# A fourth even unit moved by DMA, loads paced one behind each move, and the sum first in each turn of VectorE

## The chip, the core and the metric

The kernel runs on one core of one Trainium2 chip. A core has TensorE (PE, matrix products, with its weight loads shown as PEld), VectorE (DVE), ScalarE (ACT), GpSimd (POOL) and SyncE (SP), whose queue issues nearly all DMAs here. The metric is the device time of one execution in microseconds; the median of several executions is compared.

## The reference, cut to what matters

`x` is 2048 x 512, `adj` is 2048 x 2048, both float32.

```python
h = relu(layernorm(x))                        # layer 0
weight_q = quantised(normalised(weight))      # integers, -7 to 7
support = relu(quantised(h) @ weight_q)       # quantised again to integers, 0 to 15
x = x + c_out * (adj @ support_q)
h = relu(layernorm(x))                        # layer 1
S = (adj + adj.T) * 0.5 + eye
d = where(S.sum(axis=1) > 0, S.sum(axis=1) ** -0.5, 0)
x = x + (adj @ (d[:, None] * S * d[None, :])) @ h
```

The kernel computes the last line as `adj @ (d * (S @ (d * h)))`. The sums of S over its rows need both the row sums and the column sums of `adj`.

## The kernel before, in words

`adj` is read in 32 units of 128 rows x 1024 columns, 512 KB each. Unit u is half u % 2 of row block u // 2. TensorE needs the transposed matrix in SBUF (`at`), in float16 as a high and a low half: high = float16(256 a), low = float16(256 a - high). A unit gets there in one of two ways.

A *turned* unit goes over TensorE: `turn(u)` (L1029) makes eight transposes into a PSUM bank pair (`ps_a` and `ps_b` in alternation), ScalarE writes the high half from PSUM (`hi_turned`, L479), and VectorE takes a column sum from PSUM and writes the low half (`turned_out`, L845, with L702 and L715). ScalarE also takes the row sum in a pass of its own (`row_sum`, L462).

A *moved* unit is split before it is transposed: ScalarE writes the high half into a stage and takes the row sum on the way (`hi_rows`, L469, L476), VectorE writes the low half into the stage (`lo_rows`, L718, L720), and SP issues a DMA transpose of each from the stage to `at` (`move`, L315, L323). There are two pairs of stages, and `hi_rows` of one moved unit waits until the unit two before it has landed. All odd units from 3 to 29 and the even ones in `EVEN` (14, 18, 22) are moved. The column sums of odd units are made from a sum that GpSimd adds up in `acc` (L435 to L444), each add behind the product of some row block; those of moved even units are late column sums (L708), a VectorE pass over 2048 columns of `at`.

The first product (L1045, `layer0`) makes 16 row blocks of `adj @ support_q`; a block r is 16 column blocks with two matmuls each, and needs units 2r and, from column block 8 on, 2r + 1. It goes into one of two banks, `ps_p[r % 2]`, so block r waits until VectorE has emptied the bank of block r - 2: `x1_tile(r - 2)` (L834, L840), which adds the product to x and takes the statistics (L842, L843) for the second layer norm.

The order of the work is written out by hand. Each engine runs a loop over turns r = 1 to 13 (PE L1097, ACT L586, DVE L903, SP L355). `TURNS[r]` lists the units that TensorE turns ahead of or within block r, `MOVES[r]` those that are moved in it. In turn r VectorE does `turned_out` of the first turned unit, then `x1_tile(r - 1)`, then `lo_rows` of the first moved unit, then the rest. SP's queue is in order: it waits for the halves of a unit, issues the two transposes, and loads come between. Units 14 to 19 are loaded in one go (L353), units 20 to 23 behind the move of unit 7 (L361); from turn 8 on a load comes ahead of a move and one behind it. After the first product TensorE runs the second product (two sweeps, L1140) and the third (L1153).

Of the kernel before, what the change touches and what calls it, by code (L numbers as in the profile page):

```python
# [11 lines left out]
W = N // 2  # L12
# [11 lines left out]
GROUPS = (0, 2, 4, 8, 12, T)  # L24
LATE_GROUPS = (0, 13, T)
LATE_SUMS = (0, 2)
EVEN = (14, 18, 22)
MOVED = tuple(sorted(tuple(range(3, 30, 2)) + EVEN))
ADDED = tuple(range(1, 30, 2))
TURNED = tuple(u for u in range(UNITS) if u not in MOVED)  # L30
# [3 lines left out]
def gnn_kernel(nc, x, adj, adj_scale, weight, wgt_alpha, act_alpha, act_alpha2, out):  # L34
# [5 lines left out]
    with ctx:  # L40
# [6 lines left out]
        def sem(name):  # L47
            return ctx.enter_context(nc.semaphore(name))
# [41 lines left out]
        def late(tile, off, cols, dt):  # L90
            v = at[:, tile * PAIR + off:tile * PAIR + off + cols * (2 if dt == f32 else 1)]
            return v.bitcast(f32) if dt == f32 else v
# [2 lines left out]
        w_int = late(13, 2048, KD * D, f16)  # L95
        acc = late(15, 0, W, f32)

        def stage(u, lo):

            if u == 29:  # L100
                return late(15, 2048 + lo * W, W, f16)
            return late(14, 2048 * (MOVED.index(u) % 2) + lo * W, W, f16)
        xq = [late(12, 1024 * k, 2 * D, f16) for k in range(2)]
        sq = [late(11, 1024 * k, 2 * D, f16) for k in range(2)]
        hT = [late(10, 1024 * k, 2 * D, f16) for k in range(2)]
# [73 lines left out]
        acc_done = sem("acc_done")  # L179
        hi_ready = sem("hi_ready")  # L180
        lo_ready = sem("lo_ready")
        at_moved = [[sem(f"at_moved{k}{lo}") for lo in range(2)] for k in range(2)]
        atlo = sem("atlo")
        prod_done = sem("prod_done")
        x1_ready = sem("x1_ready")
# [84 lines left out]
        TURNS = {r: [2 * r + 4] for r in range(2, 12)}  # L270
        TURNS.update({1: [4, 6], 12: [28, "acc"], 13: [30, 31]})


        ROW_SUMS = {2: [0, 1], 4: [2, 4], "acc": []}


        MOVES = {r: [2 * r + 7] for r in range(2, 12)}
        MOVES[1] = [7, 9]
        for u in EVEN:
            MOVES[u // 2 - 4].append(u)  # L280
            TURNS[u // 2 - 2] = []

        def wait_moved(engine, u):
            k = MOVED.index(u)
            for lo in range(2):
                engine.wait_ge(at_moved[k % 2][lo], 16 * (k // 2 + 1))


        def arrivals(u):
# [2 lines left out]
        @block.sync  # L292
        def _(sp):
            def load_x(n):
                sp.dma_start(feat3[:, 2 * n:2 * n + 2, :], x_tiles[:, 2 * n:2 * n + 2, :]).then_inc(x_in[n], 16)

            def rows(u):
                sp.dma_start(unit_in(u), adj[(u // 2) * P:(u // 2 + 1) * P, (u % 2) * W:(u % 2 + 1) * W])\
                  .then_inc(arr_sem(u), 16)

            def rows_again(u):
                free_slot(before(u))
                rows(u)

            def free_slot(u):

                if u in ADDED:
                    sp.wait_ge(acc_done, ADDED.index(u) + 1)
                if u in MOVED:
                    sp.wait_ge(lo_ready, MOVED.index(u) + 1)  # L310
                else:
                    sp.wait_ge(turned, turn_no(u) + 1)
                    sp.wait_ge(rs_done, TURNED.index(u) + 1)

            def move(u):  # L315
                for lo, ready in ((0, hi_ready), (1, lo_ready)):
                    sp.wait_ge(ready, MOVED.index(u) + 1)
                    if u == 29:
                        wait_moved(sp, 25)
                        wait_moved(sp, 27)  # L320
                    elif u >= 12:
                        free_slot(waited_in(u)[lo])
                    sp.dma_start_transpose(at_half(u // 2, lo, u % 2).rearrange("p (b i) -> p b i", i=P), stage(u, lo))\  # L323
                      .then_inc(at_moved[MOVED.index(u) % 2][lo], 16)

            def store_x1(t):
                sp.wait_ge(x1_ready, t + 1)
                sp.dma_start(out_tiles[:, t:t + 1, :], feat3[:, t:t + 1, :]).then_inc(x1_stored[t], 16)

            def sums(v):  # L330
                h, j = v // T, v % T
                sp.dma_start(sum_in(v), adj[j * P:(j + 1) * P, h * W:(h + 1) * W]).then_inc(sum_arrival(v), 16)

            for h in range(2):
                sp.dma_start(w_raw[:, 2 * h * D:2 * (h + 1) * D].rearrange("p (k d) -> p k d", d=D),
                             weight.rearrange("(k p) d -> p k d", p=P)[:, 2 * h:2 * h + 2, :]).then_inc(w_in[h], 16)
            for n in range(2):
                load_x(n)
            rows(0)
            rows(1)  # L340
            for n in range(2, T // 2):
                load_x(n)
            for u in range(2, 12):
                rows(u)
            sums(0)
            sums(1)
            sp.wait_ge(hT_ps, T // 2)
            rows(12)
            rows(13)
            move(3)  # L350
            move(5)
            sp.wait_ge(sq_ready, T // 2)
            for u in range(14, 20):  # L353
                rows(u)
            for r in range(1, 12):  # L355
                if r >= 8:
                    rows_again(2 * r + 9)
                for u in MOVES[r]:
                    move(u)
                    if u == 7:  # L360
                        for w in range(AHEAD, AHEAD + 4):  # L361
                            rows_again(w)
                if r >= 8:
                    rows_again(2 * r + 8)
            for v in range(2, 6):
                free_slot(UNITS - 6 + v)
                sums(v)
            for t in range(13):
                store_x1(t)
            for v in range(6, UNITS):  # L370
                if v in (6, 7, 8):
                    store_x1(v + 7)
                sp.wait_ge(slo, v - 3)
                sums(v)

            sp.wait_ge(z_ps, 2 * B)
            for k in range(4):
                for t in range(4 * k, 4 * k + 4):
                    sp.wait_ge(x1_stored[t], 16)
                sp.dma_start(feat3[:, 4 * k:4 * k + 4, :], out_tiles[:, 4 * k:4 * k + 4, :]).then_inc(x1_back[k], 16)  # L380
            for t in range(T - 1):
                sp.wait_ge(y_out, t + 1)
                sp.dma_start(out_tiles[:, t:t + 1, :], feat3[:, t:t + 1, :]).then_inc(out_stored, 16)
            for h in range(2):
                sp.wait_ge(y_out, T + h)
                sp.dma_start(out_tiles[:, T - 1:T, h * DH:(h + 1) * DH], feat3[:, T - 1:T, h * DH:(h + 1) * DH])\
                  .then_inc(out_stored, 16)
            sp.wait_ge(out_stored, 16 * (T + 1))

        @block.gpsimd  # L390
        def _(pool):
# [42 lines left out]

            for k, u in enumerate(ADDED):  # L435
                pool.wait_ge(arr_sem(u), arrivals(u))
                if u > 5:
                    pool.wait_ge(prod_done, next(r for r in MOVES if u in MOVES[r]))
                if k == 0:
                    pool.wait_ge(lo_ready, 2)  # L440
                    nc.gpsimd.tensor_scalar(acc, unit_in(u), 0.0, 1.0, ALU.add, ALU.mult).then_inc(acc_done, 1)
                else:
                    pool.wait_ge(acc_done, k)
                    nc.gpsimd.tensor_tensor(acc, acc, unit_in(u), ALU.add).then_inc(acc_done, 1)  # L444

        @block.scalar
        def _(act):
# [21 lines left out]
            def hi_rows(u):  # L469
                k = MOVED.index(u)  # L470
                act.wait_ge(arr_sem(u), arrivals(u))
                if k < 2:
                    act.wait_ge(w_ready, 2)
                else:
                    wait_moved(act, MOVED[k - 2])
                nc.scalar.activation(stage(u, 0), unit_in(u), ACT.Copy, scale=SA, accum_out=rowsum[:, u:u + 1])\  # L476
                  .then_inc(hi_ready, 1)

# [10 lines left out]

            def turn_hi(u):  # L490
                if u == 28:
                    wait_moved(act, 25)
                    wait_moved(act, 27)
                elif u == 30:
                    wait_moved(act, 29)
                if u != "acc":
                    hi_turned(u)
# [83 lines left out]
            scale_support(7)  # L581
            hi_turned(2)
            hi_rows(5)
            for w in ROW_SUMS[2]:
                row_sum(w)
            for r in range(1, 14):  # L586
# [38 lines left out]
        def _(dve):  # L625
# [204 lines left out]
            clamp_support(7)  # L830
            lo_turned(2)
            lo_rows(5)

            def x1_tile(r):  # L834

# [66 lines left out]

            for r in range(1, 14):  # L903
                now = TURNS[r]
                for u in now[:1]:
                    turned_out(u)
                x1_tile(r - 1)
                moves = MOVES.get(r, [])
                for u in moves[:1]:
                    lo_rows(u)  # L910
# [1 line left out]
                    turned_out(u)  # L912
                for u in moves[1:]:
                    lo_rows(u)
                if r - 4 in LATE_SUMS:
                    column_sum_late(r - 4)
                for k, u in enumerate(EVEN):
                    if r == (7, 9, 12)[k]:
                        wait_moved(dve, u)
                        column_sum_late(u)  # L920
                if r == 8:
# [286 lines left out]
```

## Time and profile before

| | us |
|---|---|
| median of 3 runs | 499.73 (499.46 to 500.01) |
| the profiled execution | 499.41 |
| its span | 497.5 |
| TensorE busy | 482.9 |
| VectorE busy | 275.2 |
| ScalarE busy | 136.0 |
| GpSimd busy | 46.5 |

The span is the time from the first to the last instruction of the program that the profile shows; the profiled execution's own time lies 1.9 us above it. Times of rows count from the span's start. The granted TensorE clock is full in every slice. The first product, with the preparation of the matrix, ends at about 162 us; the second runs to about 328, the third to the end.

### The profile page before, as it was taken

The numbers are of one execution on the slowest core, as the hardware profiler recorded it, in microseconds if no ns is written. First come the engines' busy times: TensorE is split into PE (matmuls) and PEld (weight loads), VectorE is DVE, ScalarE is ACT, GpSimd is POOL, SyncE is SP. The second block draws the span as 40 slices with busy tenths as digits, with TensorE's granted clock in tenths as the row PEclk, the third lists the DMA queues.
The fourth block names the chain that finished last, engine by engine and source line by source line (L and its number), as shares of the span: only waits on it lengthen the run. The fifth ranks groups of instructions, "written<-read, shape, count | busy, mean of one in ns | idle before, by whom it ended". The sixth has DMA issues, their size and how long they took to land.

```text
span 497.5 us, 6362 instructions
## 1 busy us (share of the span) xinstructions
PE 482.9 (97%) x2390; PEld 236.6 (48%) x2390; DVE 275.2 (55%) x367; ACT 136.0 (27%) x192; POOL 46.5 (9%) x54
## 2 busy tenths in 40 slices
PE   3999998999999999999999999999999999999997
PEld 2755554445554444444444444444444444444446
DVE  6964969989999688785996777340000000000000
ACT  1796634433432343534512122140000000000000
POOL 2322932332200000000000000000000000000000
PEclk9999999999999999999999999999999999999999
DMA  8978996779677233233223231045010000100001
GB/s 296 402 315 191 303 243 130 130 172 208 152 216 288 65 106 124 87 107 104 86 89 122 88 123 42 1 134 224 22 42 21 21 21 21 42 21 21 22 21 43
DMA packets 54731, 60.56 MB, mean 122 GB/s; under 512 B 37688, under 2 KB 37944, under 8 KB 54712
## 3 DMA queue, kind: packets, MB, share of 16 engines
q1 hardware_dynamic: 54704, 60.30, 40.5%
q8 instruction: 12, 0.20, 0.2%
q14 instruction: 7, 0.06, 0.0%
q10 hardware_dynamic: 8, 0.00, 0.0%
HBM read 42.99 MB, written 8.39 MB: 103 GB/s over the span
## 4 chain that ended last, share of the span: by engine, by line
PE 84%; DVE 7%; DMA 3%; SPq 2%; ACT 1%; issue 1%; POOL 0%; ACTq 0%; DVEq 0%; POOLq 0%
PE ps_a L1163 31%; PE ps_p L1062 13%; PE ps_p L1126 7%; PE ps_a L1126 7%; PE ps_b L1126 7%; PE ps_m L1126 4%; PE ps_h L1126 4%; DMA feat<-in_x 2%; DVE at L720 2%; PE ps_b L1013 1%; PE ps_m L1062 1%; PE ps_h L1062 1%; DVE at L715 1%; DVE small L900 1%; PE ps_b L1179 1%
## 5 line engine op out<-in xcount | busy, mean ns | idle before, releaser
L1062 PE MATMUL ps_p<-small,at 128*128 128x512 f16 x448 | 100.0, 379 | 2.0 <-DVE feat L840 2.0
L982 DVE SCALAR_TENSOR_TENSOR feat<-ps_a,feat 128x512 f32<-128x512 f32 (+1 forms) x16 | 10.8, 676 | 148.7 <-PE ps_a L1163 144.2
L1163 PE MATMUL ps_a<-small,at 128*128 128x512 f16 x360 | 80.2, 379 | 0.0
L1163 PE MATMUL ps_a<-a_in,at 128*128 128x512 f16 x360 | 80.2, 379 | 0.0
L1062 PEld LDWEIGHTS ps_p<-small,at 128*128 128x128 f16 x448 | 43.6, 98 | 51.5 <-DVE feat L840 2.5
L551 ACT ACTIVATE split<-a_in 128x1024 f16<-128x1024 f32 x30 | 31.7, 1057 | 101.5 <-PE ps_p L1126 90.0
L1163 PEld LDWEIGHTS ps_a<-a_in,at 128*128 (+1 forms) x360 | 35.2, 98 | 42.5
L1163 PEld LDWEIGHTS ps_a<-small,at 128*128 (+1 forms) x360 | 35.2, 98 | 42.5
L896 DVE TENSOR_TENSOR split<-a_in,split 128x1024 f16<-128x1024 f32 x30 | 36.7, 1224 | 33.7 <-ACT split L551 33.7
L1126 PE MATMUL ps_p<-feat,split 128*128 (+1 forms) x180 | 43.9, 379 | 0.5 <-DVE small L900 0.5
L1126 PE MATMUL ps_a<-feat,split 128*128 (+1 forms) x180 | 43.8, 379 | 0.0
L1126 PE MATMUL ps_b<-feat,split 128*128 (+1 forms) x180 | 43.7, 379 | 0.0
L887 DVE TENSOR_TENSOR a_in<-a_in,at 128x1024 f32<-128x1024 f32 x30 | 36.8, 1226 | 1.0
L886 DVE SCALAR_TENSOR_TENSOR a_in<-a_in,at 128x1024 f32<-128x1024 f32 x30 | 36.5, 1218 | 0.0
L1126 PEld LDWEIGHTS ps_p<-feat,split 128*128 128x128 f16 x180 | 17.5, 98 | 22.0 <-DVE small L900 1.0
L1126 PEld LDWEIGHTS ps_a<-feat,split 128*128 128x128 f16 x180 | 17.6, 98 | 21.4 <-issue 0.5
L1126 PEld LDWEIGHTS ps_b<-feat,split 128*128 128x128 f16 x180 | 17.6, 98 | 21.2
L1126 PE MATMUL ps_m<-feat,split 128*128 (+1 forms) x90 | 24.3, 379 | 0.0
L1126 PE MATMUL ps_h<-feat,split 128*128 (+1 forms) x90 | 24.3, 379 | 0.0
L444 POOL TENSOR_TENSOR at<-at 128x1024 f32<-128x1024 f32 x8 | 21.2, 2648 | 18.4 <-PE ps_p L1062 17.8
L444 POOL TENSOR_TENSOR at<-at,a_in 128x1024 f32<-128x1024 f32 x6 | 15.2, 2537 | 25.4 <-PE ps_p L1062 19.2
L720 DVE SCALAR_TENSOR_TENSOR at<-at 128x1024 f16<-128x1024 f32 x10 | 14.2, 1428 | 4.7 <-ACT at L476 4.7
(179 smaller groups left out, 432.5 us busy)
## 6 DMA issues: line engine op xcount, KB each, us to landing
a_in<-in_adj SPq DMA_DIRECT2D x46, 512.0 KB, 3.9
at<-in_adj SPq DMA_DIRECT2D x16, 512.0 KB, 10.0
out<-feat SPq DMA_DIRECT2D x31, 256.0 KB, 4.2
feat<-in_x SPq DMA_DIRECT2D x8, 512.0 KB, 10.8
feat<-out SPq DMA_DIRECT2D x4, 1024.0 KB, 9.3
at<-in_L_gnn_weight SPq DMA_DIRECT2D x2, 512.0 KB, 3.8
at<-at SPq DMA_TRANSPOSE x34, 3.3
split<-in_adj SPq DMA_DIRECT2D x1, 512.0 KB, 16.2
```

What stands on the lines that cost most here:

```text
L444: nc.gpsimd.tensor_tensor(acc, acc, unit_in(u), ALU.add).then_inc(acc_done, 1)
L551: nc.scalar.activation(part(v % 2, 0), sum_in(v), ACT.Copy).then_inc(shi, 1)
L715: nc.vector.scalar_tensor_tensor(at_half(u // 2, 1, u % 2), turn_bank(u)[:, :], SA, at_half(u // 2, 0, u % 2), ALU.mult, ALU.subtract).the ...
L720: nc.vector.scalar_tensor_tensor(stage(u, 1), unit_in(u), SA, stage(u, 0), ALU.mult, ALU.subtract)\
L886: link(nc.vector.scalar_tensor_tensor(u3, u3, SA, at_across(h, 0, j), ALU.mult, ALU.add))
L887: last = nc.vector.tensor_tensor(u3, u3, at_across(h, 1, j), ALU.add)
L896: nc.vector.tensor_tensor(part(v % 2, 1), sum_in(v), part(v % 2, 0), ALU.subtract).then_inc(slo, 1)
L900: nc.vector.scalar_tensor_tensor(z_part(t, 1), BANK[t % B], cz[:, t:t + 1], z_part(t, 0), ALU.mult, ALU.subtract).then_inc(z_ready, 1)
L982: nc.vector.scalar_tensor_tensor(out, products, 1.0 / (SA * SZ), out, ALU.mult, ALU.add).then_inc(y_out, 1)
L1062: last = nc.tensor.matmul(l0_bank(r), at_block(r, lo, j), small[:, j * D:(j + 1) * D], start=(j == 0 and lo == 0), stop=(j == T - 1 and lo ...
L1126: last = nc.tensor.matmul(BANK[t], part(k, lo)[:, t * P:(t + 1) * P], g_part(j, g_lo), start=(first and lo + g_lo == 0), stop=False)
L1163: last = nc.tensor.matmul(BANK[n], at_block(t, lo, j), z_part(j, z_lo), start=(j == 0 and lo + z_lo == 0), stop=(j == T - 1 and lo == 1))
```

## The change

Unit 10 joins `EVEN`: it is no longer turned (turn 3 has no turned unit) but moved. There are three pairs of stages in place of two, the third in row tile 15 (`stage_no`). Unit 7 is moved ahead of the loop, and the moved units are put anew on the turns: in turns 3 to 7 the even ones come one turn later than before, but for 22. On SP's queue only units 14 and 15 are loaded in one go; each of 16 to 23 is loaded behind one move (`LOADS`). GpSimd's adds keep their turns by a table (`ADD_AT`), the one of unit 7 without a wait for a product; its first waits for the low half of unit 7. ScalarE takes the row sum of unit 1 in turn 1. VectorE does `x1_tile(r - 1)` first in turn r, ahead of `turned_out`, and the late sums of units 0 and 2 come one turn earlier; that of unit 10 is in turn 5.

```diff
-EVEN = (14, 18, 22)
+EVEN = (10, 14, 18, 22)
...
+        def stage_no(u):
+            return (MOVED.index(u) - len(MOVED)) % 3
+
         def stage(u, lo):
-            if u == 29:
-                return late(15, 2048 + lo * W, W, f16)
-            return late(14, 2048 * (MOVED.index(u) % 2) + lo * W, W, f16)
+            k = stage_no(u)
+            return late(14 + k // 2, 2048 * (k % 2 if k < 2 else 1) + lo * W, W, f16)
...
-        ROW_SUMS = {2: [0, 1], 4: [2, 4], "acc": []}
-        MOVES = {r: [2 * r + 7] for r in range(2, 12)}
-        MOVES[1] = [7, 9]
         for u in EVEN:
-            MOVES[u // 2 - 4].append(u)
             TURNS[u // 2 - 2] = []
+        ROW_SUMS = {2: [0], 4: [1, 2, 4], "acc": []}
+        MOVES = {1: [9], 2: [10, 11], 3: [13], 4: [14, 15], 5: [17], 6: [18, 19], 7: [21, 22], 8: [23], 9: [25],
+                 10: [27], 11: [29]}
+        ADD_AT = {u: r for r in MOVES for u in MOVES[r]}
...
             sp.wait_ge(sq_ready, T // 2)
-            for u in range(14, 20):
-                rows(u)
+            rows(14)
+            rows(15)
+            move(7)
+            LOADS = {9: [16], 10: [17], 11: [18], 13: [19], 14: [20], 15: [21], 17: [22], 18: [23]}
             for r in range(1, 12):
                 if r >= 8:
                     rows_again(2 * r + 9)
                 for u in MOVES[r]:
                     move(u)
-                    if u == 7:
-                        for w in range(AHEAD, AHEAD + 4):
+                    for w in LOADS.get(u, []):
+                        if w < AHEAD:
+                            rows(w)
+                        else:
                             rows_again(w)
...
-                if u > 5:
-                    pool.wait_ge(prod_done, next(r for r in MOVES if u in MOVES[r]))
+                if u in ADD_AT:
+                    pool.wait_ge(prod_done, ADD_AT[u])
                 if k == 0:
-                    pool.wait_ge(lo_ready, 2)
+                    pool.wait_ge(lo_ready, 3)
...
-                if k < 2:
+                if k < 3:
                     act.wait_ge(w_ready, 2)
                 else:
-                    wait_moved(act, MOVED[k - 2])
+                    wait_moved(act, MOVED[k - 3])
...
             hi_rows(5)
+            hi_rows(7)
...
             lo_rows(5)
+            lo_rows(7)
...
             for r in range(1, 14):
                 now = TURNS[r]
+                x1_tile(r - 1)
                 for u in now[:1]:
                     turned_out(u)
-                x1_tile(r - 1)
...
-                if r - 4 in LATE_SUMS:
-                    column_sum_late(r - 4)
+                if r - 3 in LATE_SUMS:
+                    column_sum_late(r - 3)
                 for k, u in enumerate(EVEN):
-                    if r == (7, 9, 12)[k]:
+                    if r == (5, 7, 9, 12)[k]:
```

## Rows read from the trace of the kernel before

**Rows 1.** The page: busy time of each engine, and the chain that ended last.

```profile
PE 482.9 (97%) x2390; PEld 236.6 (48%) x2390; DVE 275.2 (55%) x367; ACT 136.0 (27%) x192; POOL 46.5 (9%) x54
...
PE 84%; DVE 7%; DMA 3%; SPq 2%; ACT 1%; issue 1%; POOL 0%; ACTq 0%; DVEq 0%; POOLq 0%
```

**Rows 2.** Waits of TensorE: total us, times, longest.

```profile
PE ps_p L1062 <- DVE feat L840: 2.0, 1, 2.0
...
PE ps_p L1126 <- DVE small L900: 0.5, 1, 0.5
```

**Rows 3.** Timeline of TensorE, 44 to 165: start, us, instruction, idle before.

```profile
61.49 1.04 PE L1041 MATMUL ps_a<-ident,at 128*128 128x128 f32 x8
62.36 7.07 PE L1062 MATMUL ps_p<-small,at 128*128 128x512 f16 x32
...
70.14 7.07 PE L1062 MATMUL ps_p<-small,at 128*128 128x512 f16 x32
79.19 7.08 PE L1062 MATMUL ps_p<-small,at 128*128 128x512 f16 x32 [1.97 <-DVE feat L840]
...
131.93 1.90 PE L1062 MATMUL ps_p<-small,at 128*128 128x512 f16 x8
...
139.72 1.04 PE L1041 MATMUL ps_a<-ident,a_in 128*128 128x128 f32 x8
...
155.28 7.07 PE L1062 MATMUL ps_m<-small,at 128*128 128x512 f16 x32
```

**Rows 4.** Timeline of VectorE, 68 to 80.

```profile
76.12 1.22 DVE L702 TENSOR_REDUCE colp<-ps_b 128x8 f32<-128x1024 f32 x1
...
78.39 0.74 DVE L840 SCALAR_TENSOR_TENSOR feat<-ps_p,cst,feat 128x512 f32<-128x512 f32 x1
```

**Rows 5.** Timeline of ScalarE, 68 to 80.

```profile
71.20 1.06 ACT L476 ACTIVATE at<-at 128x1024 f16<-128x1024 f32 x1 [7.10 <-DMA at<-at]
...
74.86 1.00 ACT L487 ACTIVATE at<-ps_b 128x1024 f16<-128x1024 f32 x1
```

**Rows 6.** SP's queue: timeline, 51 to 64 and 133 to 137; line 323 (ns min/median/max).

```profile
59.02 1.97 SPq L298 DMA_DIRECT2D a_in<-in_adj  x4
61.04 8.07 SPq L323 DMA_TRANSPOSE at<-at  x2
...
135.29 0.52 SPq L298 DMA_DIRECT2D a_in<-in_adj  x1
...
L323 SPq DMA_TRANSPOSE at<-at x34: 1231/1265/6357, 38.0 to 134.0; - x34
...
DMA to landing us min/median/max: 3.0/3.3/9.1
```

**Rows 7.** Lines 708 and 840: ns min/median/max, first and last start.

```profile
L708 DVE TENSOR_REDUCE colp<-at x5: 2277/2279/2280, 81.1 to 140.0; 128x8 f32<-128x2048 f16 x5
...
L840 DVE SCALAR_TENSOR_TENSOR feat<-ps_p,cst,feat x14: 735/742/745, 51.8 to 152.8; 128x512 f32<-128x512 f32 x14
```

**Rows 8.** Stretches: length, then busy us of PE, PEld, DVE, ACT, POOL.

```profile
46.00:102.90 56.90, 54.93 (x279) 27.80 (x278) 46.01 (x48) 27.46 (x46) 28.75 (x12) 1.00 0.89 202
102.90:148.30 45.40, 45.40 (x236) 23.49 (x234) 44.83 (x46) 17.70 (x27) 8.71 (x4) 1.00 0.75 184
```

**Rows 9.** Timeline of VectorE, 44 to 64.

```profile
44.87 1.22 DVE L720 SCALAR_TENSOR_TENSOR at<-at 128x1024 f16<-128x1024 f32 x1
...
53.44 2.49 DVE L720 SCALAR_TENSOR_TENSOR at<-at 128x1024 f16<-128x1024 f32 x1
...
63.12 2.12 DVE L720 SCALAR_TENSOR_TENSOR at<-at 128x1024 f16<-128x1024 f32 x1
```

**Rows 10.** Timeline of GpSimd, 44 to 72.

```profile
52.48 2.37 POOL L444 TENSOR_TENSOR at<-at 128x1024 f32<-128x1024 f32 x1 [0.17 <-POOL at L444]
```

**Rows 11.** Timeline of VectorE, 131 to 149.

```profile
131.13 0.74 DVE L840 SCALAR_TENSOR_TENSOR feat<-ps_p,cst,feat 128x512 f32<-128x512 f32 x1
...
132.73 1.19 DVE L720 SCALAR_TENSOR_TENSOR at<-a_in,at 128x1024 f16<-128x1024 f32 x1
```

**Rows 12.** Waits of ScalarE.

```profile
ACT at L476 <- DMA at<-at: 22.9, 9, 7.1
```

More of the change, by code:

```diff
@@ L181, in gnn_kernel @@
         lo_ready = sem("lo_ready")
-        at_moved = [[sem(f"at_moved{k}{lo}") for lo in range(2)] for k in range(2)]
+        at_moved = [[sem(f"at_moved{k}{lo}") for lo in range(2)] for k in range(3)]
         atlo = sem("atlo")
@@ L271, in gnn_kernel @@
         TURNS.update({1: [4, 6], 12: [28, "acc"], 13: [30, 31]})
-        ROW_SUMS = {2: [0, 1], 4: [2, 4], "acc": []}
-        MOVES = {r: [2 * r + 7] for r in range(2, 12)}
-        MOVES[1] = [7, 9]
         for u in EVEN:
-            MOVES[u // 2 - 4].append(u)
             TURNS[u // 2 - 2] = []
+        ROW_SUMS = {2: [0], 4: [1, 2, 4], "acc": []}
+        MOVES = {1: [9], 2: [10, 11], 3: [13], 4: [14, 15], 5: [17], 6: [18, 19], 7: [21, 22], 8: [23], 9: [25],
+                 10: [27], 11: [29]}
+        ADD_AT = {u: r for r in MOVES for u in MOVES[r]}
         def wait_moved(engine, u):
             k = MOVED.index(u)
+            same = [w for w in MOVED[:k + 1] if stage_no(w) == stage_no(u)]
             for lo in range(2):
-                engine.wait_ge(at_moved[k % 2][lo], 16 * (k // 2 + 1))
+                engine.wait_ge(at_moved[stage_no(u)][lo], 16 * len(same))
         def arrivals(u):
@@ L318, in move @@
                     if u == 29:
-                        wait_moved(sp, 25)
-                        wait_moved(sp, 27)
+                        wait_moved(sp, MOVED[-3])
+                        wait_moved(sp, MOVED[-2])
                     elif u >= 12:
@@ L323, in move @@
                     sp.dma_start_transpose(at_half(u // 2, lo, u % 2).rearrange("p (b i) -> p b i", i=P), stage(u, lo))\
-                      .then_inc(at_moved[MOVED.index(u) % 2][lo], 16)
+                      .then_inc(at_moved[stage_no(u)][lo], 16)
             def store_x1(t):
@@ L491, in turn_hi @@
                 if u == 28:
-                    wait_moved(act, 25)
-                    wait_moved(act, 27)
+                    wait_moved(act, MOVED[-3])
+                    wait_moved(act, MOVED[-2])
                 elif u == 30:
```

## The prediction

> **What bounds the kernel now.** I read the page first. TensorE is busy 482.9 us of a span of 497.5, and the chain that ended last is TensorE for 84% [rows 1]. So time is won only where TensorE has less to do or stops waiting. TensorE's own waits come next: after the first 23 us there are two, 2.0 us in the first product and 0.5 us in the second [rows 2]. The timeline of TensorE puts the 2.0 us wait between the fifth and sixth row blocks of the first product. Block r=4 starts at 70.14. A block is 32 matmuls; from 62.36 to 70.14 lie one block and one turn of 0.87, so it takes 6.91 us (0.216 a matmul). Block 4 therefore ends at 77.05, by the timeline's last end 77.2, and block 5 starts at 79.19 [rows 3].
>
> Why it waits is read backwards from VectorE. Block 5 needs bank r%2, which `x1_tile(3)` frees; that instruction ran at 78.39 [rows 4], although its product was complete at 69.3 (62.36 + 6.91 [rows 3]). In VectorE's program it stood behind the low halves of units 13 and 14 and behind `turned_out(12)`, 76.12 to 78.39 [rows 4]. These waited for ScalarE, where `hi_rows(13)` sat idle for 7.10 us until 71.20 for a stage to come free, with the high half of unit 12 (74.86) behind it [rows 5]. The stage was held by unit 9's transposes: issued from 61.04 on, right behind the four loads of units 20 to 23 issued from 59.02 on, they kept SP's queue for 8.07 us, until 69.1; one transpose is otherwise issued in 1.27 and landed in 3.3 [rows 6]. One long chain, then: four loads ahead of a move, a stage, ScalarE, VectorE, a bank.
>
> **The change part by part.** Each time is the profiled execution's (499.41 us; span 497.5 and 1.9 around it). The median of the runs shown, 499.73, lies 0.32 above it.
>
> *Unit 10 is moved.* TensorE loses the eight transposes of `turn(10)`. From their start to the next matmul is 62.36 - 61.49 = 0.87 us [rows 3] (the 1.04 shown overlaps its neighbour). TensorE is gapless there, so this counts in full: -0.87. ScalarE: `hi_turned` (1.00 for its like) and `row_sum`, a pass of the same width, become one `hi_rows` (1.06) [rows 5]: less. VectorE: `turned_out(10)`, 2.27 from 76.12 to 78.39 for its like [rows 4], becomes `lo_rows` (1.22 [rows 9]) and a late column sum of 2.28 [rows 7]; with the 0.08 by which neighbours overlap, +1.1 us. SP: two more transposes, 1.27 us of issue each [rows 6]; its other issues stay the same in number. Cover: before 102.9, VectorE is idle 56.90 - 46.01 = 10.9 us [rows 8]. If that cover were gone the 1.1 us would land on TensorE.
>
> *The 2.0 us wait.* Two edits act on it, and either seems nearly enough. Loads 16 to 23 now come singly behind moves, so no move lies behind more than two loads; three stage pairs instead of two let ScalarE run one unit further ahead. And `x1_tile(3)` is first in its turn. Working forward from the low half of unit 5 (44.87 to 46.09 [rows 9]), with steps from start to start of 1.1 us for a low half, 1.6 for `x1_tile` with its statistics (131.13 to 132.73 [rows 11]), 2.27 for `turned_out`, 2.2 for a late sum, and with ScalarE's and TensorE's hand-overs where they come later: `lo_rows(7)` ends about 47.2, `x1_tile(0)` 48.8, `turned_out(4)` 51.1; `lo_rows(9)` and `turned_out(6)` end by 56.7, `x1_tile(1)` 58.3, `turned_out(8)` 60.6, the low halves of 10 and 11 by 65.4 (with 2.5 us of waiting for GpSimd in it), `x1_tile(2)` 67.1, low half 13 68.3, late sum 70.5. `x1_tile(3)` frees its bank at 71.3. Block 5 would start at 77.2 - 0.87 = 76.3, so it has 5 us to spare. Gain: -1.97 [rows 3]. From below it could be nothing, if VectorE is late elsewhere (rival 1); more than 1.97 it cannot give, as there is no more idle time there. I take all of it.
>
> *What could be late next.* Unit 10 must be landed at 76.3. Its high half is ready at 57 (ScalarE, behind `hi_turned(8)`), its low at 61.8; two transposes of 3.3 us [rows 6] make 65 (by a worst landing of 9.1, 71). A block reads its odd unit 16 matmuls (3.5 us) after its start. So unit 9: 57.5 against 70.14 - 0.87 + 3.5 = 72.7; before, 71.2 (the end of ScalarE's wait [rows 5]) against 73.6. Unit 11: 68.5 against 79.7. Moves 14 and 18 come one turn later than before, about 80 and 96, for blocks 7 and 9, which start at 91 and 106. Other banks: `x1_tile(2)` at 66.1 for block 4 at 69.3; `x1_tile(5)` at 88.2 for block 7. Their slack is 2.7 us and more even where VectorE runs without a pause. So rows, SP order and the third stage I cost at nothing; each only has to be early. Bounds: -0 to +2.84 together, the latter if one of them gave back everything.
>
> *GpSimd.* `acc` now starts behind the low half of unit 7, about 1.1 us later, and its adds run back to back into the time of the low halves. A row shows what this costs: the low half at 53.44 took 2.49 us against 1.22, while an add of 2.37 us ran from 52.48 to 54.85; one more low half took 2.12, at 63.12 [rows 9, 10]. The Trainium skill, "SBUF — State Buffer", section "SBUF: two separate sides", says that VectorE, in an instruction with two SBUF inputs, and GpSimd take a shared port pair as an exclusive lock, and the loser blocks for the whole of the other's instruction; the row agrees (54.85 plus about 1.1 is 55.93). By that rule up to three more low halves could meet an add before block 7, 3 x 1.3 = 3.9 us of VectorE; by the rows it is two in that stretch. Two (2.5 us) are in the times above, and they leave 5 us free; the sum does not change.
>
> *From 102.9 on.* VectorE is busy 44.83 of 45.40 us [rows 8]: as much a bound as TensorE. `x1_tile(10)` ended at 131.87, and block 12, which needs its bank, began at 131.93 [rows 3, 11]. If TensorE came 2.84 us earlier and VectorE did not, it would wait there. But `x1_tile(10)` now stands ahead of `turned_out(26)` (2.3 us), and VectorE enters this stretch earlier: turn 8 starts with `x1_tile(7)` at 98 to 100 instead of 102.9 with `turned_out(20)`. Carried on without a pause, the pessimistic sum gives `x1_tile(10)` 126.7 against 129.1, and `x1_tile(13)` 150.4 instead of 152.8 [rows 7]; the optimistic one 124 and 148.5. After that block 15 (155.28 + 7.07 = 162.35 before [rows 3]) and `x1_tile(15)` go by TensorE; the second and third products follow it at their old pace.
>
> **Sum.** -0.87 - 1.97 = -2.84. Profiled execution 499.41 - 2.84 = 496.57; from the median 499.73, 496.9.
>
> **Rivals.**
> 1. *VectorE lags, or the bank is still late.* For: its full load after 102.9. Against: 10.9 us of idle before, and `x1_tile` first. Price: 0.5 to 2.3 of the 2.84 comes back, at block 7, 10 or 12: 497.4 to 499.2. "The change doesn't do what it says" is the end of this: only the turn goes, 499.73 - 0.87 = 498.9.
> 2. *The gain is all given back at the turn of unit 30.* The load of unit 30 is issued behind the low move of unit 29, at 135.29 [rows 6], and the turn began at 139.72 [rows 3], some 4.4 us later: it began as its rows came. The low half of unit 29 ends at 133.92 [rows 11]. If it does not end earlier, the turn stays at 139.72 however early TensorE comes: 499.4 to 500.0. Against: VectorE's lead of 2.4 to 4.6 us in the sum above.
> 3. *Slower, by the same place.* If the low half of 29 ends later than 133.92, every microsecond of it is one of the kernel. The added 1.1 us of VectorE work with one or two more collisions of 1.3 us would do it if nothing of the idle time before 102.9 absorbed them: 499.7 + 1.1 = 500.8 to 499.7 + 1.1 + 2.6 = 503.4. For: the late sum and low half of unit 10 go to the busiest engine there; the loads of units 20 to 23, now behind moves 14, 15, 17 and 18, make ScalarE and so VectorE later if one of those moves is. Against: turns 3 to 7 have slack in every step above.
>
> **How the numbers follow.** Forecast: 0.68, with 496.3 to 497.4. Rival 1: 0.15 (faster). Rival 2: 0.09 (same). Rival 3: 0.08 (slower). A change of 0.2%, 1.0 us, is about what a measurement can tell. Faster 0.68 + 0.15 = 0.83. The range runs from 496.2 (the runs differ by 0.3 around the sum) up into rival 1 to 498.8, which leaves out its end and rivals 2 and 3, about 0.2.
>
> **What would show it.** In TensorE's waits the 2.0 us entry on `feat` is gone, and no wait on a DMA or on `feat` above 0.3 us has come. Block 15 ends near 159.5. Transposes number 36, all but the first landing in 3 to 6 us, with no move that keeps SP's queue for 8. ScalarE's wait for moves (22.9 us [rows 12]) falls to a third or less. VectorE shows 6 late column sums (L708's like) where it had 5, and 11 from PSUM where it had 12. Wrong would be: a pause of TensorE before block 7, 10 or 12 (rival 1), or ahead of the turn of unit 30 with VectorE gapless from 100 on (rivals 2 and 3).

## The result, and the profile after

| | median | runs |
|---|---|---|
| before | 499.67 | 498.79 to 502.02 (6) |
| after | 496.88 | 496.19 to 497.05 (6) |

The ratio is 0.9937, interval 0.9919 to 0.9956: 2.8 us faster. The profiled execution took 497.05 with a span of 494.9. Measured a second time, on another chip, it took 496.52 (ratio 0.9952, 0.9938 to 0.9966).

The page, answering to [rows 1]: TensorE has eight transposes less, and the chain is now TensorE for 92% in place of 84%.

```profile
PE 480.7 (97%) x2382; PEld 234.8 (47%) x2382; DVE 275.2 (56%) x367; ACT 134.2 (27%) x191; POOL 45.8 (9%) x54
...
PE 92%; DVE 3%; DMA 2%; ACT 1%; SPq 1%; issue 1%; POOL 0%; ACTq 0%
```

The waits of TensorE, answering to [rows 2]. The 2.0 us on `feat` is gone. The 1.4 us on L695 lies at 20 us, ahead of all that was changed; it was 0.4 in the profile before, and 0.2 to 1.5 in the other profiles below, so it varies from execution to execution.

```profile
PE ps_b L1024 <- DVE at L695: 1.4, 1, 1.4
...
PE ps_p L1137 <- DVE small L911: 0.5, 1, 0.5
```

The timeline of TensorE, 44 to 165, answering to [rows 3]. Blocks 4 and 5 are now one run of 64 matmuls from 69.77, and no line ahead of the second product has an idle time.

```profile
45.56 1.04 PE L1052 MATMUL ps_b<-ident,at 128*128 128x128 f32 x8
...
55.09 13.98 PE L1073 MATMUL ps_p<-small,at 128*128 128x512 f16 x64
68.90 1.04 PE L1052 MATMUL ps_a<-ident,at 128*128 128x128 f32 x8
69.77 13.98 PE L1073 MATMUL ps_p<-small,at 128*128 128x512 f16 x64
...
137.17 1.04 PE L1052 MATMUL ps_b<-ident,a_in 128*128 128x128 f32 x8
...
159.64 1.46 PE L1137 MATMUL ps_a<-feat,split 128*128 128x512 f16 x6
```

I use one measure of this timeline for every kernel below, **the stretch**: from the start of the turn of unit 4 to the first matmul of the second product. It leaves out what single executions do at the start. Before it is 162.19 - 45.06 = 117.13; after, 159.64 - 45.56 = 114.08, and 114.08 again in the second measurement. So 3.05 us went here. (The stretches below are taken from unrounded times, so the last digit can differ by one from the rows.)

VectorE, answering to [rows 4] and [rows 9]: `x1_tile(3)` is at 69.74 instead of 78.39. The first line holds two low halves (units 10 and 11) of 1.61 and 3.37 us, lengthened by adds of GpSimd.

```profile
59.42 4.90 DVE L730 SCALAR_TENSOR_TENSOR at<-at 128x1024 f16<-128x1024 f32 x2
64.25 0.74 DVE L851 SCALAR_TENSOR_TENSOR feat<-ps_p,cst,feat 128x512 f32<-128x512 f32 x1
...
65.84 1.78 DVE L730 SCALAR_TENSOR_TENSOR at<-at 128x1024 f16<-128x1024 f32 x1
...
69.74 0.73 DVE L851 SCALAR_TENSOR_TENSOR feat<-ps_p,cst,feat 128x512 f32<-128x512 f32 x1
```

SP's queue, answering to [rows 6] (line 328, then its landing; the load of unit 30), ScalarE's wait for moves, answering to [rows 12], and VectorE's share of two stretches, answering to [rows 8]:

```profile
L328 SPq DMA_TRANSPOSE at<-at x36: 1231/1266/3677, 38.5 to 126.4; - x36
DMA to landing us min/median/max: 3.0/4.3/6.5
```

```profile
127.72 0.52 SPq L303 DMA_DIRECT2D a_in<-in_adj  x1
```

```profile
ACT at L485 <- DMA at<-at: 4.7, 2, 4.3
```

```profile
46.00:100.06 54.06, 54.06 (x275) 27.28 (x274) 51.09 (x50) 25.81 (x46) 28.63 (x12) 1.00 1.06 214
100.06:145.46 45.40, 45.40 (x236) 23.63 (x235) 41.51 (x51) 17.80 (x28) 8.17 (x4) 1.00 0.76 191
```

The median landing of a move is 4.3 us where it was 3.3, since more moves now lie behind one load; the worst is 6.5 instead of 9.1. That the shorter worst landing is what removed TensorE's wait is not shown: with the third stage pair alone (below) the worst stays 9.0 and the wait goes too. ScalarE waits 4.7 us for moves instead of 22.9. The load of unit 30 is issued 7.6 us earlier. VectorE has 3.9 us of room in 45.4 where it had 0.6.

### The profile page after: what moved, and what is told of

Its sections match the earlier page's. It is cut to its first block, busy times and chain, and to the rows that moved or that the text cites. A ratio compares the mean times of both kernels' runs of the same rounds, so it can differ in the third digit from the quotient of the medians.

```text
span 494.9 us, 6346 instructions
## 1 busy us (share of the span) xinstructions
PE 480.7 (97%) x2382; PEld 234.8 (47%) x2382; DVE 275.2 (56%) x367; ACT 134.2 (27%) x191; POOL 45.8 (9%) x54
## 4 chain that ended last, share of the span: by engine, by line
PE 92%; DVE 3%; DMA 2%; ACT 1%; SPq 1%; issue 1%; POOL 0%; ACTq 0%
PE ps_a L1174 31%; PE ps_p L1073 20%; PE ps_p L1137 7%; PE ps_a L1137 7%; PE ps_b L1137 7%; PE ps_m L1137 4%; PE ps_h L1137 4%; DMA feat<-in_x 2%; PE ps_b L1024 1%; PE ps_m L1073 1%; PE ps_h L1073 1%; PE ps_a L1052 1%; DVE small L911 1%; PE ps_b L1190 1%; PE ps_a L1190 1%; PE ps_b L1052 1%
## 5 line engine op out<-in xcount | busy, mean ns | idle before, releaser
L730 DVE SCALAR_TENSOR_TENSOR at<-at 128x1024 f16<-128x1024 f32 x11 | 16.9, 1562 | 0.0
```

Source lines behind the costliest of these rows:

```text
L730: nc.vector.scalar_tensor_tensor(stage(u, 1), unit_in(u), SA, stage(u, 0), ALU.mult, ALU.subtract)\
```

## The experiments

Each was timed beside the kernel before (499.52, 499.65 and 499.29 in three sets, each set on a chip of its own), so ratios compare best; the stretch is from its one profile.

| kernel | median (runs) | ratio to before, interval | stretch |
|---|---|---|---|
| before, `x1_tile` first | 503.05 (502.2 to 504.3) | 1.0067, 1.0049 to 1.0085 | 119.97 |
| before, third stage pair | 497.96 (496.7 to 501.8) | 0.9977, 0.9955 to 0.9999 | 115.10 |
| the first, adds behind low halves | 502.42 (499.5 to 505.6) | 1.0067, 1.0044 to 1.0089 | 119.90 |
| after, unit 10 turned | 498.02 (497.4 to 499.7) | 0.9971, 0.9957 to 0.9984 | 115.10 |
| the same, `x1_tile` second | 498.74 (498.5 to 500.1) | 0.9983, 0.9970 to 0.9997 | 116.25 |
| after, `x1_tile` second | 498.95 (497.3 to 501.5) | 0.9980, 0.9960 to 0.9999 | 115.21 |
| after, two stage pairs | 502.61 (500.9 to 504.8) | 1.0059, 1.0038 to 1.0081 | 121.34 |
| after, again | 496.52 (496.4 to 497.8) | 0.9952, 0.9938 to 0.9966 | 114.08 |
| after, two late sums more | 498.47 (497.9 to 499.5) | 0.9969, 0.9956 to 0.9983 | 116.42 |
| the same, loads ahead of the move | 498.58 (498.1 to 499.4) | 0.9982, 0.9970 to 0.9995 | 115.79 |
| after, unit 26 moved too | 496.67 (495.1 to 501.3) | 0.9951, 0.9923 to 0.9979 | 114.53 |
| the same, loads ahead of the last move | 495.64 (495.3 to 495.8) | 0.9928, 0.9914 to 0.9942 | 113.21 |

### One part of the change alone

**`x1_tile` first, in the kernel before.**

```diff
             for r in range(1, 14):
                 now = TURNS[r]
+                x1_tile(r - 1)
                 for u in now[:1]:
                     turned_out(u)
-                x1_tile(r - 1)
```

> The kernel before with one edit: x1_tile(r - 1) ahead of turned_out in VectorE's turn; unit 10 turned, two stage pairs, loads in one go as before. Theory (the wait before block 5 has two remedies, and each is enough alone): VectorE is free for x1_tile(3) after the low half of unit 14, at 76.2; it frees the bank at 76.9, before block 5 comes at 77.05. The whole wait goes: -2.1 us, about 497.6, no entry on feat in TensorE's waits, while ScalarE still waits some 20 us for moves. Rival (the late moves are the cause, and only paced loads take it away): x1_tile(3) comes no earlier than the late halves let it, under 0.7 us gained, 499.0 or more. Second rival: TensorE then waits ahead of the turn of unit 30, whose rows landed 0.1 us before their use: nothing gained, 499.7.

Measured: 503.05, 3.5 us slower. No expectation had this time. The wait before block 5 was gone, as the theory said (`x1_tile(3)` ended at 76.6), but TensorE stood 3.3 us for the rows of unit 24. In the profile of this kernel, the first two fences are VectorE's low halves (L720) and GpSimd's adds, 83 to 101; the third is SP's queue, 105 to 114; the fourth TensorE's timeline.

```profile
83.07 0.74 DVE L840 SCALAR_TENSOR_TENSOR feat<-ps_p,cst,feat 128x512 f32<-128x512 f32 x1
84.67 4.31 DVE L720 SCALAR_TENSOR_TENSOR at<-at 128x1024 f16<-128x1024 f32 x2
...
92.74 2.88 DVE L720 SCALAR_TENSOR_TENSOR at<-at 128x1024 f16<-128x1024 f32 x1
...
99.34 3.19 DVE L720 SCALAR_TENSOR_TENSOR at<-a_in,at 128x1024 f16<-128x1024 f32 x1
```

```profile
84.41 2.35 POOL L444 TENSOR_TENSOR at<-at 128x1024 f32<-128x1024 f32 x1 [4.55 <-PE ps_p L1062]
92.19 2.35 POOL L444 TENSOR_TENSOR at<-at,a_in 128x1024 f32<-128x1024 f32 x1 [5.42 <-PE ps_p L1062]
99.09 2.35 POOL L444 TENSOR_TENSOR at<-at,a_in 128x1024 f32<-128x1024 f32 x1 [4.55 <-PE ps_p L1062]
```

```profile
107.26 4.83 SPq L323 DMA_TRANSPOSE at<-at  x2
112.19 1.02 SPq L298 DMA_DIRECT2D a_in<-in_adj  x2
```

```profile
116.97 1.97 PE L1041 MATMUL ps_a<-ident,a_in 128*128 128x128 f32 x8 [3.31 <-DMA a_in<-in_adj]
118.73 7.71 PE L1062 MATMUL ps_p<-small,at 128*128 128x512 f16 x32
```

GpSimd's add starts with the end of a product. With the wait before block 5 gone, TensorE's products end about 2 us earlier, and the adds start as much earlier. VectorE, which has no idle time from 76 to 100, did not move with them: the low half of unit 17 starts at 84.67 here and at 84.90 in the kernel before, where the add came behind it:

```profile
84.90 2.33 DVE L720 SCALAR_TENSOR_TENSOR at<-at 128x1024 f16<-128x1024 f32 x2
```

```profile
86.40 3.03 POOL L444 TENSOR_TENSOR at<-at 128x1024 f32<-128x1024 f32 x1 [6.70 <-PE ps_p L1062]
```

So three low halves now start 0.25 to 0.55 us behind an add's start, and take about 3 us instead of 1.2 (the 4.31 are two, of 3.17 and 1.21). The low halves hold the stages, the stages hold the high halves, and the load of unit 24 stands in SP's queue behind the low half of unit 23 (107.26 to 112.09). It was issued at 112.2 and landed at 116.9. Of the 2.8 us by which the stretch is longer, 1.3 are the longer wait (3.31 for 1.97) and 1.5 a lower clock behind it (last section).

**The collisions taken away from that kernel.**

```diff
-                    pool.wait_ge(prod_done, next(r for r in MOVES if u in MOVES[r]))
+                    r = next(r for r in MOVES if u in MOVES[r])
+                    pool.wait_ge(prod_done, r)
+                    pool.wait_ge(lo_ready, MOVED.index(max(MOVES[r])) + 1)
```

> The kernel before with x1_tile first (the run that came out 3.5 us slower), and each of GpSimd's adds from unit 7 on made to wait for the low halves of its turn as well as for the product. Theory (x1_tile first puts the low half 1.6 us behind the product's end, just when GpSimd's add of 2.35 us starts; three low halves took 2.9 to 3.2 us instead of 1.2 that way, at 84.7, 92.7 and 99.3; they held the stages, these the moves, and these the load of unit 24, for which TensorE waited 3.3 us): low halves at 1.2 to 1.8 us, moves 21 and 22 some 3 to 5 us earlier, TensorE's wait ahead of the turn of unit 24 under 1 us; 498 to 500. Rival (the late load comes from SP's order and the two stages, whatever GpSimd does): TensorE waits 2.5 us or more there, 502 to 503.

Measured: 502.42, no better, and in the range that the rival gave, though for another reason. The first half of the theory held: no low half above 1.62 us in the profile (the first fence), the low half of unit 22 at 97.4 instead of 102.5, and no wait at the turn of unit 24. But the edit made a wait of its own: `acc` was complete too late, and TensorE waited 3.2 us for it (the second fence). So the chain from the collisions to the late rows is supported, and its price can't be read from this total.

```profile
L722 DVE SCALAR_TENSOR_TENSOR at<-at x10: 1192/1218/1621, 45.0 to 90.8; 128x1024 f16<-128x1024 f32 x10
```

```profile
PE ps_b L1043 <- POOL at L446: 3.2, 1, 3.2
```

**The third stage pair alone, in the kernel before.** The diff is that of `stage_no`, `stage`, `at_moved`, `wait_moved` and `hi_rows` in the change, of which this is the part in `hi_rows`.

```diff
-                if k < 2:
+                if k < 3:
                     act.wait_ge(w_ready, 2)
                 else:
-                    wait_moved(act, MOVED[k - 2])
+                    wait_moved(act, MOVED[k - 3])
```

> The kernel before with a third pair of stages and nothing else: loads in one go, two moves to the turns as before, turned_out ahead of x1_tile, unit 10 turned. Two stages in the changed kernel cost 5.7 us, so the third pair is suspected to be the part that carries the gain. Theory (the third pair alone frees ScalarE from unit 9's late landing): hi_rows(13) starts near 64 instead of 71, x1_tile(3) frees its bank by 76, the wait before block 5 goes: 2 us less, 497.6, with up to 0.8 given back at block 12 or the rows of unit 28 or 30. Rival (the loads in one go hold the moves whatever the stages): a wait of 1 us or more stays at block 5, 498.7 to 499.7.

Measured: 497.96; the stretch is 115.10, 2.03 shorter than before, and TensorE has no wait in it. ScalarE's `hi_rows(13)` started at 62.84 (71.20 before [rows 5]), behind nothing but its own program:

```profile
62.84 1.05 ACT L480 ACTIVATE at<-at 128x1024 f16<-128x1024 f32 x1
...
70.40 1.06 ACT L480 ACTIVATE at<-at 128x1024 f16<-128x1024 f32 x1 [5.39 <-DMA at<-at]
```

This part alone takes the wait away, with the loads in one go as before and a worst landing of 9.0 us. Its margins are thin: `x1_tile(3)` ended at 75.78, 0.6 us ahead of block 5, and `x1_tile(10)` at 129.20, just as block 12 started (129.26). In the changed kernel the two are 6.2 and 7.4 us ahead. Its executions scatter (496.7 to 501.8; the profiled one was the fastest), and the median gains 1.3 us, not 2.

### One part of the change taken back

**Unit 10 turned again.**

```diff
-EVEN = (10, 14, 18, 22)
+EVEN = (14, 18, 22)
...
-        MOVES = {1: [9], 2: [10, 11], ...
+        MOVES = {1: [9], 2: [11], ...
...
-            LOADS = {9: [16], 10: [17], 11: [18], 13: [19], 14: [20], 15: [21], 17: [22], 18: [23]}
+            LOADS = {9: [16], 11: [17], 13: [18], 14: [19], 15: [20], 17: [21], 18: [22], 19: [23]}
...
```

> The changed kernel with unit 10 turned again, the rest as in the change (x1_tile first, three stage pairs, each load behind one move, from 17 on one move later than with unit 10 moved). Theory (moving a unit is worth the eight transposes that TensorE loses and nothing else): 0.87 us more than the changed kernel, 497.75, TensorE without a wait in the first product. Rival (the move of unit 10 also costs VectorE 1.1 us and SP two transposes that TensorE pays for in part): less than 0.5 us more.

Measured: 498.02. The stretch is 1.02 longer than after, against 0.87; TensorE shows no wait in it. As the theory said: the unit is worth its transposes, and VectorE's 1.1 us for it is paid from idle time. The stretch is that of the third stage pair alone (115.10). So the paced loads and `x1_tile` first, taken together, shorten nothing in the profiled executions beyond what the third pair does; what they add is margin. The spread is smaller too, 497.4 to 499.7 instead of 496.7 to 501.8, in 12 and 11 executions on two chips. Whether unit 10 could be moved with the third pair and nothing else was not run.

**The same with `x1_tile` second: pacing and stages without the rest.**

> The changed kernel with unit 10 turned and turned_out ahead of x1_tile again: what is left of the change is unit 7 ahead of the loop, the loads behind single moves, the third stage pair and the late sums of 0 and 2 a turn earlier. Theory (each remedy is enough alone): ScalarE no longer waits for unit 9's stage, turned_out(12) is done by 73 to 75 and x1_tile(3) frees its bank by 76; 497.7 as without unit 10, at most 0.3 more at block 12, where x1_tile stands behind turned_out again. Rival (x1_tile first is what counts, VectorE is the bound): a wait of 1 to 2 us stays, at block 5 or at block 12: 498.7 to 499.7.

Measured: 498.74, the stretch 1.15 longer than with `x1_tile` first. The waits are 0.3 us for the rows of unit 28 and 0.4 on `feat` at block 12. The theory had no wait at block 5, rightly, and 0.3 at block 12; the median, 1.0 above its 497.7, is at the foot of the rival's range, though the rival's wait of 1 to 2 us is not there.

**`x1_tile` second in the changed kernel.**

> The changed kernel with one edit undone: turned_out ahead of x1_tile, as before. Theory: banks are freed 2.3 us later in turns with a turned unit (x1_tile(3) then near 72.8, x1_tile(10) near 124.3), and both stay ahead of their blocks (76.7 and 129.4): no change, 496.9. Rival (VectorE as the bound, with 1.1 us more work than before): TensorE waits 0.5 to 2 us at blocks 4, 5 or 12: 497.4 to 498.9.

Measured: 498.95, and executions from 497.3 to 501.5. The profile, one of the faster executions, shows the wait that the rival named, at block 12, where the bank is freed behind `turned_out(26)`:

```profile
130.03 1.90 PE L1073 MATMUL ps_p<-small,at 128*128 128x512 f16 x8 [0.83 <-DVE feat L851]
```

By the ratios `x1_tile` first is worth 1.4 to 2.1 us here, by the stretch 1.1, though it made the kernel before slower.

**Two stage pairs.**

```diff
-            return (MOVED.index(u) - len(MOVED)) % 3
+            return MOVED.index(u) % 2
...
-                if k < 3:
+                if k < 2:
...
-                    wait_moved(act, MOVED[k - 3])
+                    wait_moved(act, MOVED[k - 2])
```

> The changed kernel with two pairs of stages in place of three (unit 29 in row tile 15 as before). Theory (the loads are what kept the stages; with one load between moves a move lands 4 to 6 us from its issue and two pairs are nearly enough): high halves of 13, 15 and 17 come 1 to 5 us later, VectorE has that much to spare in turns 3 to 5: 496.9 to 497.5, no wait of TensorE above 0.5. Rival (the third pair is what freed ScalarE): hi_rows waits 10 us or more for moves, x1_tile late at block 5 to 12, 498 or more.

Measured: 502.61. The rival came, further out than its 498: ScalarE waits 30 us for moves, and `x1_tile(7)` is late for block 9. The first fence is ScalarE's waits for moves (4.7 us with three pairs); the second VectorE's timeline, waiting for ScalarE's high half of unit 22; the third TensorE's timeline; the fourth the stretches behind the first pause, where the third number from the right is the granted clock.

```profile
ACT at L486 <- DMA at<-at: 30.0, 11, 7.3
```

```profile
103.74 1.23 DVE L731 SCALAR_TENSOR_TENSOR at<-a_in,at 128x1024 f16<-128x1024 f32 x1 [3.81 <-ACT at L486]
...
107.08 0.74 DVE L852 SCALAR_TENSOR_TENSOR feat<-ps_p,cst,feat 128x512 f32<-128x512 f32 x1
```

```profile
107.88 8.77 PE L1074 MATMUL ps_p<-small,at 128*128 128x512 f16 x32 [2.41 <-DVE feat L852]
118.31 1.09 PE L1053 MATMUL ps_b<-ident,a_in 128*128 128x128 f32 x8 [1.66 <-DMA a_in<-in_adj]
```

```profile
108.00:113.00 5.00, 5.00 (x16) 1.90 (x15) 4.97 (x6) 1.15 (x2) 1.82 (x1) 0.66 0.70 151
113.00:118.00 5.00, 3.65 (x17) 1.47 (x15) 4.90 (x5) 0.96 (x1) 1.34 (x1) 1.00 0.88 203
```

### The room that is left

**VectorE given 4.6 us more.**

```diff
+                if r in (9, 11):
+                    for _ in range(1):
+                        column_sum_late(10)
```

> The changed kernel with VectorE taking the late sum of unit 10 again at the end of turns 9 and 11: 2 x 2.28 = 4.6 us more of VectorE, to measure its room from 100 us on (it was idle for 3.9 us of 45.4 there). Theory (x1_tile first and the earlier entry give VectorE some 7 us before block 12): no change, 496.9 to 497.2. Rival (VectorE is at the bound after 100 us as it was before, the gain hangs by a thread): 1 to 4 us slower, a wait on feat at block 12 or 13 or on the rows of unit 30.

Measured: 498.47, the stretch 2.3 longer. The theory fell, and the rival had the price, with the wait at another unit. TensorE waited 1.8 us for the rows of unit 28. In the changed kernel they landed at 124.2, 4.3 us ahead of their use; with the load behind the low half of unit 27, VectorE's delay went straight to it (low half at 120.7 instead of 117.4, and it met an add: 3.39 us).

**The same with SP's second load of a turn ahead of the move.**

```diff
                 for u in MOVES[r]:
+                    if r >= 8 and u == MOVES[r][-1]:
+                        rows_again(2 * r + 8)
                     move(u)
...
-                if r >= 8:
-                    rows_again(2 * r + 8)
```

> The changed kernel with the two extra late sums of VectorE (4.6 us, at the end of turns 9 and 11; that run came out 1.6 us slower, TensorE waiting 1.8 us for the rows of unit 28) and the second load of turns 8 to 11 (units 24, 26, 28, 30) ahead of the turn's move instead of behind it. Theory (VectorE's extra time reached TensorE only through SP's order, load behind low half): the rows of 28 land some 5 us before their use, no wait there, 496.9 to 497.3. Rival (VectorE itself is late for the banks): a wait of 1 us or more on feat in its place, 498 or more.

Measured: 498.58, no faster than with the load behind. The wait for rows went, as the theory said; one of 1.5 us came ahead of the turn of unit 30, for the PSUM bank that `turned_out(28)` frees. So both: the load's place was the first limit, VectorE itself the next, and its room from turn 9 on is under 4.6 us.

```profile
PE ps_b L1055 <- DVE at L725: 1.5, 1, 1.5
```

**The changed kernel again**, on the chip of the run above and the last run below.

> The changed kernel itself, on the chip of the two runs that follow, as their yardstick: 496.9, within 0.3 of its first time. A wait of TensorE at the turn of unit 28, which came up in two variants of it, is not expected: its rows landed 4.3 us ahead of their use.

Measured: 496.52, 0.4 below its first time; in its first product only a wait of 0.2 us at a load remains.

**Unit 26 moved as well.**

```diff
-EVEN = (10, 14, 18, 22)
+EVEN = (10, 14, 18, 22, 26)
...
-                 10: [27], 11: [29]}
+                 10: [26, 27], 11: [29]}
...
-                    if r == (5, 7, 9, 12)[k]:
+                    if r == (5, 7, 9, 11, 12)[k]:
```

> The changed kernel with unit 26 moved too (in turn 10, ahead of 27; its late sum in turn 12, that of 22 in turn 11). Theory (a unit off TensorE is worth its eight transposes as long as VectorE and SP have room; in the changed kernel x1_tile(10) is done 7 us before block 12 wants its bank): -0.87 us, 496.0. Rival (from turn 10 on SP's order binds: the load of unit 28 stands behind moves 26 and 27, that of 30 behind 29): the turn of 28 or 30 waits for its rows, 496.9 or more.

Measured: 496.67, but from 495.1 to 501.3. The fastest executions have the theory's gain; the profile (497.99) shows the rival's wait, 1.1 us for the rows of unit 28, now behind two moves. With the load put ahead of the turn's last move, as in the edit above:

> The changed kernel with unit 26 moved as well and the second load of turns 8 to 11 ahead of the turn's last move. The version with the load behind both moves waited 1.1 us for the rows of unit 28, 496.7 with a spread of 495.1 to 501.3. Theory (the rest is SP's order): no wait for rows, 0.87 less than the changed kernel, 496.0, and a spread of under 1 us. Rival (the spread comes from VectorE meeting GpSimd's adds): still up to 500 in single executions.

Measured: 495.64 (495.3 to 495.8), 0.88 under the changed kernel on the same chip; the stretch is 113.21, 0.87 shorter. This is the fastest version; it was executed only five times, so its narrow spread is weaker evidence than its trace. Its TensorE has no idle time between 44 and the second product:

```profile
113.57 13.98 PE L1073 MATMUL ps_p<-small,at 128*128 128x512 f16 x64
127.38 1.04 PE L1052 MATMUL ps_a<-ident,a_in 128*128 128x128 f32 x8
...
158.50 1.46 PE L1137 MATMUL ps_a<-feat,split 128*128 128x512 f16 x6
```

## Why the prediction was right

*The sum.* Forecast -2.84, measured -2.8 in the medians (3.1 and 2.4 us by the two ratios). Both terms are seen in the trace, in place. The stretch became 3.05 shorter. The turn of unit 10 is worth 0.87 by its row and 1.02 in the stretch with it turned; unit 26 gave 0.87. The wait was mis-sized a little: 1.97 is the idle time that the row shows, counted from the modelled end of a pipelined matmul; from start to start, block 4 to block 5 took 79.19 - 70.14 = 9.05 instead of 6.91 [rows 3], which is 2.14. That makes 3.01. The profiled executions differ by only 2.36: the one of after entered the stretch 0.5 us later, and the remaining 0.2 us lie outside its span.

*The chain behind the wait* (four loads, a move, a stage, ScalarE, VectorE, a bank) is shown from the stage on: a third stage alone takes the wait away. That the four loads made the move slow is read from [rows 6]; no run took the loads alone away.

*"Two edits act on it, and either seems nearly enough"* holds for that one wait and misleads for the kernel. Either edit alone removed it, but `x1_tile` first alone made the kernel 3.5 us slower. The third stage pair, which I had costed at nothing ("each only has to be early"), carries the most: alone it takes the wait away, and without it the changed kernel takes 502.6, 5.7 us more, twice the 2.84 that I had as the bound for rows, SP order and third stage together (1.7 of the 5.7 is the lower clock behind its first pause). The deadlines that I checked were those of single moves; that a stage waited for delays the next high half, that the next low half, and through SP's order the next load, I did not follow beyond turn 3. Nor did I ask what else moves when TensorE comes 2 us earlier, which is how `x1_tile` first alone lost.

*GpSimd.* I put in two meetings of a low half with an add, 2.5 us. The profile has six low halves lengthened, 5.1 us in all; four of them, 3.8 us, lie ahead of block 7, so the 3.9 that I had named as the most was nearer than the 2.5 that I took for two. The slack covered it: `x1_tile(3)` ended at 70.5 (71.3 forecast), `x1_tile(13)` at 149.5 (148.5 to 150.4). `x1_tile(10)`, at 122.0, was earlier than either of my sums (124 and 126.7). That the times fit although GpSimd cost VectorE more than I took is partly luck: by `x1_tile(1)` the sum was already 1 us too long (58.3, measured 57.2).

*The rivals.* None came, but their mechanisms are real and close: `turned_out` ahead of `x1_tile` brings rival 1 at block 12; 4.6 us more of VectorE brings a wait for rows behind a low half, as in rivals 2 and 3, at unit 28 rather than 30. The 0.08 for a slower kernel was not idle: one part of the change made alone, or one left out, gives one.

*The signs.* They held, but for one detail: no wait on `feat`, block 15 ended at 159.8 (159.5 forecast), 36 transposes, ScalarE's wait at a fifth, 6 late column sums and 11 from PSUM. The worst landing was 6.5 us, where I had 3 to 6.

## What to carry to other kernels

A queue that issues in order turns a late half into a late load, and the load into a stall several turns on: put loads that don't need the half ahead of it, and give the stage one more buffer than the steady state needs. When a wait is removed, all that hangs on that engine's events comes earlier too, and may land beside work of a third engine that did not move: check what it will run beside. Test the parts of a change alone, since here one that loses 3.5 us alone gains 1.1 to 2.1 in company. Compare trace against trace from start to start of a fixed stretch, and time each version often enough to see its spread: with unit 26 moved, the other order of the loads left the fastest execution where it was (495.1 against 495.3), while the five executions had nothing like the 501.3 of the first order.

## What the runs showed of the hardware

*Some pauses of TensorE cost more than themselves.* After 1.97 us idle in the kernel before, the granted clock stayed at 1.00 (2.4 GHz) and the next block took its usual 7.08 us [rows 3]. After 2.41 us idle with two stage pairs it was 0.66 on average over the next 5 us, and the block took 8.77: 1.70 more. After 3.24 us with the adds behind low halves it was 0.61 over 4 us. After 3.31 us with `x1_tile` first, the clock was at 0.50 (1.2 GHz) for 2 us; from the start of the turn to the next matmul took 1.76 instead of 0.87, and the block 7.71:

```profile
117.00:119.00 2.00, 2.00 (x9) 1.82 (x10) 2.00 (x3) 0.03 (x1) 0.65 (x1) 0.50 1.01 215
119.00:122.00 3.00, 3.00 (x13) 1.23 (x12) 3.00 (x3) 3.00 (x5) 1.70 (x1) 0.83 0.70 102
```

So the wait that this change removed was the longest seen in the first product that cost only itself. Some executions of the kernel before seem to have lost more: of its 81 in the three sets, ten have a mean granted clock of 0.996 or 0.997 over the execution, where the profiled one has 1.00, among them all six that took over 501.5 us. Which pause did it in them is not shown, since none was profiled. No execution of the changed kernel is below 0.999.

*A low half and an add that meet wait for each other's end.* The low half of unit 10 started at 59.42, inside the add of 57.59 to 59.95, and ended at 61.03, 1.08 us behind the add's end. The low half of unit 11 started at 60.95, inside the add of 60.12 to 63.24, and ended at 64.32, again 1.08 behind. That is nearly the whole of its own 1.22. The two adds that started inside these low halves, at 60.12 and 63.41, took 3.12 and 3.13 instead of 2.36, and ended 2.2 us behind the low half's end. VectorE's row of unit 11, and the timeline of GpSimd, 58 to 72, answering to [rows 10]:

```profile
60.95 3.37 DVE L730 SCALAR_TENSOR_TENSOR at<-at 128x1024 f16<-128x1024 f32 x1
```

```profile
57.59 2.36 POOL L453 TENSOR_TENSOR at<-at 128x1024 f32<-128x1024 f32 x1 [0.17 <-POOL at L453]
60.12 3.12 POOL L453 TENSOR_TENSOR at<-at 128x1024 f32<-128x1024 f32 x1 [0.17 <-POOL at L453]
63.41 3.13 POOL L453 TENSOR_TENSOR at<-at 128x1024 f32<-128x1024 f32 x1 [0.17 <-POOL at L453]
```
